# A two-layer graph network: the first expert layer scatters its rows by token, combining becomes plain, and work moves between stages

## The reference

```python
xn = LN(x)
# layer 0: attention over edges (8 heads) + linear attention, then 2 of 8 experts
g = leaky_relu(xr[dst] + xl[src], 0.2)          # xl, xr: projections of xn
alpha = einsum(g, att) + log(edge_weight)       # softmax over the edges of each dst
x = x + segment_sum(xl[src] * softmax(alpha), dst) + bias + linear_attention(xn)
t = LN(x)
mask = one_hot(top_k(t @ Wg + bg, 2)).sum()
x = x + sum_e mask[e] * (gelu(t @ W1[e] + b1[e]) @ W2[e] + b2[e])
# layer 1: two graph convolutions + linear attention with an MLP, then 1 of 8 experts
xn = LN(x)
x = x + relu(gcn(relu(gcn(xn, W1)), W2)) + mix(xn)
x = x + nan_to_num(capacity_expert(x))          # at most 977 rows per expert
```

## Time and profile before

| | |
|---|---|
| median of 3 runs | 5924.41 us (5920.71 to 5925.23) |
| profiled execution | 5924.94 us, its span 5923.2 us |
| TensorE busy | 4048.7 us, 68% of the span |
| GpSimd busy | 3097.9 us, 52% |
| VectorE busy | 2628.5 us, 44% |
| ScalarE busy | 1112.7 us, 19% |
| mean granted TensorE clock | 0.749 of full speed |
| moved by DMA | 602.72 MB, mean 102 GB/s |

### The profile page before, as it was taken

How to read it: one execution, slowest core, us unless ns; L and a number is a source line. 1 busy time by engine, 2 the same in 40 slices (tenths; PEclk the granted TensorE clock), 3 DMA queues, 4 the chain that set the end, 5 groups by cost and what they waited for, 6 DMA issues and landing times. The chain is left out here.

```text
span 5923.2 us, 82263 instructions
## 1 busy us (share of the span) xinstructions
PE 4048.7 (68%) x19460; PEld 3300.3 (56%) x19461; DVE 2628.5 (44%) x5923; ACT 1112.7 (19%) x2524; POOL 3097.9 (52%) x3161
## 2 busy tenths in 40 slices
PE   4788999999469965089934555555455555592998
PEld 3577888888447744067734444444444444461665
DVE  5333333333689975034444434444433334342443
ACT  0122222222159921022210000000000000021121
POOL 1166767676248831500066777777677777603111
PEclk9889888888679985599955556666555555555999
DMA  5365555565248843342242111111211111122220
GB/s 197 94 183 182 180 178 181 177 181 177 70 157 273 272 135 108 122 125 64 62 122 54 32 32 33 33 33 30 44 33 32 33 32 34 28 72 81 84 79 31
DMA packets 414884, 602.72 MB, mean 102 GB/s; under 512 B 97612, under 2 KB 305118, under 8 KB 413351
## 3 DMA queue, kind: packets, MB, share of 16 engines
q1 hardware_dynamic: 283019, 348.08, 17.8%
q0 software_dynamic: 107056, 200.91, 14.7%
q10 hardware_dynamic: 24732, 52.87, 2.6%
HBM read 392.17 MB, written 221.97 MB: 104 GB/s over the span
## 5 line engine op out<-in xcount | busy, mean ns | idle before, releaser
L1867 POOL DMA_INDIRECT big<-t_d,src_tiles x1564 | 1497.9, 958 | 552.2 <-issue 462.5
L2090 PE MATMUL v_bank<-big,v_oh 128*128 x3328 | 682.9, 391 | 926.4 <-POOLq L1863 861.6
L2090 PEld LDWEIGHTS v_bank<-big,v_oh 128*128 128x128 f32 x3328 | 649.6, 299 | 1004.0 <-issue 1004.0
L640 POOL DMA_INDIRECT se_xj<-xl_d,se_idx x832 | 833.8, 1002 | 371.9 <-issue 193.0
L1945 DVE TENSOR_TENSOR big<-big,v_bank 128x64 f32 x1664 | 367.8, 221 | 1158.0 <-PE v_bank L2090 922.8
L737 PE MATMUL se_z_ps<-big,se_oht 128*128 x1664 | 543.4, 455 | 73.1 <-issue 45.7
L683 DVE TENSOR_TENSOR se_z<-se_z_ps,se_xj 128x528 f32<-128x528 f32 x416 | 293.3, 705 | 584.8 <-DMA se_xj<-xl_d,se_idx 450.3
L976 POOL TENSOR_TENSOR ae_v<-ae_v,ex 128x1792 f32<-128x1792 f32 x104 | 334.2, 3217 | 243.0 <-DMA ae_v<-xj_d 242.8
L759 PEld LDWEIGHTS se_al_ps<-atta,se_zt 128*128 128x128 f32 x3328 | 459.3, 214 | 0.0
L759 PE MATMUL se_al_ps<-atta,se_zt 128*128 128x8 f32 x3328 | 444.5, 260 | 0.0
L1017 PE MATMUL ae_bank<-ae_v,ae_oh 128*128 128x266 f32 x1664 | 401.1, 396 | 51.4 <-DVE big L1001 37.4
(11 more groups left out here) (406 smaller groups left out, 5916.6 us busy)
## 6 DMA issues: line engine op xcount, KB each, us to landing
xj_d<-se_xj SPq DMA_DIRECT2D x208, 528.0 KB, 3.4
ae_v<-xj_d SPq DMA_DIRECT2D x208, 528.0 KB
big<-t_d,src_tiles POOLq DMA_INDIRECT x1564
buf_d<-e_blank ACTq DMA_DIRECT2D x4, 4112.0 KB, 35.7
e_xs<-buf_d SPq DMA_DIRECT2D x106, 128.0 KB
y_d<-e_y SPq DMA_DIRECT2D x106, 128.0 KB
se_xj<-xl_d,se_idx POOLq DMA_INDIRECT x832, 3.1
v_xt<-xnt_d SPq DMA_DIRECT2D x98, 128.0 KB
```

Of the source, the lines that this page charges most:

```text
L640: nc.gpsimd.indirect_dma_start(half_of(u)[:, k, :], None, table, bass.IndirectOffsetOnAxis(ap=idx[:, u, k:k + 1], axis=0)).then_inc(landed ...
L1867: nc.gpsimd.indirect_dma_start(rows[:, t % RING, :], None, table, bass.IndirectOffsetOnAxis(ap=m.srct[:, t:t + 1], axis=0)).then_inc(lande ...
L2090: last = nc.tensor.matmul(bank[u][:, k * MH:(k + 1) * MH], oh[:, u, k, :], of_block(rows, at[k]), start=True, stop=True)
```

## The change

- Start: the nine projection weights are loaded by `load_projections` on ScalarE's queue in `edge_steps`, behind x and ahead of the zeroing. The read-back of the tables moves to the start of `project_nodes` on SyncE. `buf0_d` has rows of TW = 258: the last two columns, 1e6 in the blank, are to hold a token and an expert.
- Score stage: TensorE reads four block numbers at every second `expand` instead of two at each.
- Normalise stage: GpSimd makes the blank tile and SyncE blanks `buf1_d` there (and the pad rows of `y0_d`).
- Route, layer 0: each scattered row carries its token and its first expert; `erow` keeps the expert of each tile as floats on all partitions; `m.back` is gone.
- First experts: VectorE's `index` computes, two tiles ahead of the bias, where each row of a tile goes: its token, plus NP = 6272 if the tile's expert isn't the row's first. GpSimd scatters each y tile to `y0_d` (2 x NP rows) with that index. SyncE only loads; a load waits for the index of the tile that held the buffer. Rows of a blank have an index out of bounds and aren't written. The blanking is gone.
- Combine: SyncE loads each group's rows of both halves of `y0_d` in two plain DMAs; GpSimd does nothing.

The diff, cut to its core (lines "..." stand for what is left out; left out are declarations, and the context):

```diff
@@ -177,13 +178,16 @@
-        rowsin, stored, floats = m.sem("es_rowsin"), m.sem("es_stored"), m.sem("es_floats")
+        rowsin, floats = m.sem("es_rowsin"), m.sem("es_floats")
...
+        m.weighted = nc.alloc_semaphore(name="weighted")
+        stored = m.stored
...
-        zeros = m.ex[:, 2 * NT:2 * NT + ZT * D]
+        zeros = m.ex[:, 2 * NT:2 * NT + ZT * TW]
...
@@ -213,17 +217,11 @@
-                sp.dma_start(m.key_d.rearrange("(j p) e -> p j e", p=P), fd[:, :, :]).then_inc(stored, 16)
+                sp.dma_start(m.key_d.rearrange("(j p) e -> p j e", p=P), fd[:, :, :]).then_inc(m.keyed, 16)
...
-                sp.wait_ge(stored, 64)
-                sp.dma_start(m.btab, m.btab_d[0:NS].rearrange("(a n) -> a n", a=1)).then_inc(stored, 16)
-                sp.dma_start(m.stab, m.stab_d[0:NS].rearrange("(a n) -> a n", a=1)).then_inc(stored, 16)
-                ends_of_groups = m.need_d[0:NS].rearrange("(g k) -> k g", k=GS)[GS - 1:GS, :]
-                sp.dma_start(m.need, ends_of_groups, allow_slow_non_contiguous=True).then_inc(stored, 16)
-                sp.wait_ge(stored, 112)
...
@@ -232,13 +230,14 @@
-                act.wait_ge(zeroset, 1)
+                load_projections(act, m, a)
+                act.wait_ge(zeroset, 2)
...
-                    act.dma_start(m.buf0_d[b0 * P:b1 * P, :].rearrange("(p b) d -> p (b d)", p=P), zeros[:, 0:(b1 - b0) * D]).then_inc(zeroed, 16)
+                    act.dma_start(m.buf0_d[b0 * P:b1 * P, :].rearrange("(p b) d -> p (b d)", p=P), zeros[:, 0:(b1 - b0) * TW]).then_inc(zeroed, 16)
...
@@ -267,7 +266,9 @@
-                nc.vector.memset(zeros, 0.0).then_inc(zeroset, 1)
+                blank = zeros.rearrange("p (b d) -> p b d", d=TW)
+                nc.vector.memset(blank[:, :, 0:D], 0.0).then_inc(zeroset, 1)
+                nc.vector.memset(blank[:, :, D:TW], 1.0e6).then_inc(zeroset, 1)
...
@@ -419,6 +420,27 @@
+def load_projections(act, m, a):
+    wl, wr, wlt, wrt, bl, br, bcol, attc = m.projections
+    for out, w in ((wl[:, :, 0:D], "L0_gnn_W_l"), (wr[:, :, 0:D], "L0_gnn_W_r"), (wlt[:, :, :], "W_lT"),
...
+        act.dma_start(out, a[w].rearrange("(c p) n -> p c n", p=P)).then_inc(m.weighted, 16)
+    for out, w in ((bl[:, 0:D], "L0_gnn_b_l"), (br[:, 0:D], "L0_gnn_b_r")):
+        act.dma_start(out, a[w].partition_broadcast(P)).then_inc(m.weighted, 16)
+    for out, w in ((bcol[:, 0, :], "L0_gnn_b_l"), (bcol[:, 1, :], "L0_gnn_b_r")):
+        act.dma_start(out, a[w].rearrange("(c p) -> p c", p=P), allow_slow_non_contiguous=True).then_inc(m.weighted, 16)
+    act.dma_start(attc[:, :], a["L0_gnn_att"].rearrange("h c -> (h c)").rearrange("(c p) -> p c", p=P), allow_slow_non_contiguous=True).then_inc(m.weighted, 16)
...
@@ -454,14 +473,11 @@
-                for out, w in ((wl[:, :, 0:D], "L0_gnn_W_l"), (wr[:, :, 0:D], "L0_gnn_W_r"), (wlt[:, :, :], "W_lT"),
...
-                    sp.dma_start(out, a[w].rearrange("(c p) n -> p c n", p=P)).then_inc(s["weights"], 16)
...
+                sp.wait_ge(m.stored, 48)
+                sp.dma_start(m.btab, m.btab_d[0:NS].rearrange("(a n) -> a n", a=1)).then_inc(m.stored, 16)
+                sp.dma_start(m.stab, m.stab_d[0:NS].rearrange("(a n) -> a n", a=1)).then_inc(m.stored, 16)
+                ends_of_groups = m.need_d[0:NS].rearrange("(g k) -> k g", k=GS)[GS - 1:GS, :]
+                sp.dma_start(m.need, ends_of_groups, allow_slow_non_contiguous=True).then_inc(m.stored, 16)
...
@@ -476,6 +492,7 @@
+                sp.wait_ge(m.stored, 96)
...
@@ -491,7 +508,8 @@
-                dve.wait_ge(s["weights"], 16 * 9)
+                dve.wait_ge(m.weighted, 16 * 9)
+                dve.wait_ge(m.keyed, 16)
...
@@ -732,9 +752,10 @@
-                    blocks = blocks_of(nc, m, mybir.EngineType.PE, q * 2, 2)
+                    if v % 2 == 0:
+                        blocks[:] = blocks_of(nc, m, mybir.EngineType.PE, q * 2, 4)
...
-                        last = nc.tensor.matmul(z_ps[v % 2][:, i, 0:LW], oht[:, u, k + i, :], of_block(m.xr, blocks[i]),
+                        last = nc.tensor.matmul(z_ps[v % 2][:, i, 0:LW], oht[:, u, k + i, :], of_block(m.xr, blocks[2 * (v % 2) + i]),
...
@@ -787,6 +809,21 @@
+            @block.gpsimd
+            def _(pool):
+                nc.gpsimd.memset(blank[:, :, 0:RW - 1], 0.0).then_inc(s["blank"], 1)
+                nc.gpsimd.memset(blank[:, :, RW - 1:RW], 1.0e6).then_inc(s["blank"], 1)
+            @block.sync
+            def _(sp):
+                sp.wait_ge(s["blank"], 2)
+                slots = m.buf1_d.rearrange("(q p b) d -> q p b d", p=P, b=16)
+                for q in range(NE * CT // 16):
+                    sp.dma_start(slots[q], blank[:, :, :].to_broadcast([P, 16, RW])).then_inc(s["blanked"], 16)
+                for e in range(2):
+                    sp.dma_start(m.y0_d[e * NP + N:(e + 1) * NP, :], blank[0:NP - N, 0, 0:D]).then_inc(s["blanked"], 16)
+                sp.wait_ge(s["blanked"], NE * CT + 32)
...
@@ -1331,8 +1368,8 @@
                     if layer == 1:
...
-                        pool.wait_ge(s["t_ready"], 2 * (g + 1))
-                        pool.sem_inc(s["issued"], 1)
+                    pool.wait_ge(s["t_ready"], 2 * (g + 1))
+                    pool.sem_inc(s["issued"], 1)
                     pool.wait_ge(s["indexed"], pairs * (g + 1))
...
@@ -1366,6 +1403,7 @@
+                    c.did(V.tensor_scalar(first[:, :], m.tmp1[:, :], float(NE), None, ALU.add))
...
@@ -1456,9 +1493,9 @@
-                    if v % 7 == 0 and layer == 1:
-                        V.tensor_copy(disp[:, v // 7, :, 2 * D], m.prob[:, bass.ds(g * 7, 7)]).then_inc(s["t_ready"], 1)
-                        V.tensor_copy(disp[:, v // 7, :, 2 * D + 1], token[:, bass.ds(g * 7, 7)]).then_inc(s["t_ready"], 1)
+                    if v % 7 == 0:
+                        for at, what in ((RW - 2, m.prob), (RW - 1, token)) if layer == 1 else ((TW - 2, token), (TW - 1, first)):
+                            V.tensor_copy(disp[:, v // 7, :, at], what[:, bass.ds(g * 7, 7)]).then_inc(s["t_ready"], 1)
...
@@ -1528,14 +1565,14 @@
-        xs, xt = sb("xs", [P, 2, D]), sb("xt", [P, 2, D])
+        xs, xt = sb("xs", [P, 2, TW]), sb("xt", [P, 2, D])
+        which, idx = sb("which", [P, T0]), sb("idx", [P, T0], U32)
...
-        blank = sb("blank", [P, 1, RW])
...
-                                           "y_made y_ready blank blanked").split()}
+                                           "y_made y_ready chosen indexed issued").split()}
...
@@ -1544,18 +1581,21 @@
                 def load(j, u, r):
...
+                        sp.wait_ge(s["indexed"], j - 1)
...
-                def store(j, u, r):
-                    sp.wait_ge(s["y_ready"], j + 1)
-                    sp.dma_start(m.y0_d[bass.ds(j * P, P), :], y[:, u, :]).then_inc(y_out[u], 16)
-                pipeline(sp, T0, 2, (0, load), (6, store))
-                for u in range(2):
-                    sp.wait_ge(y_out[u], 16 * T0 // 2)
+                pipeline(sp, T0, 2, (0, load))
...
+                def index(j, u, r):
+                    dve.wait_ge(x_in[u], 16 * (r + 1))
+                    V.tensor_scalar(which[:, bass.ds(j, 1)], xs[:, u, TW - 1:TW], m.erow[:, bass.ds(j, 1)], float(NP),
+                                    ALU.not_equal, ALU.mult).then_inc(s["chosen"], 1)
+                    dve.wait_ge(s["chosen"], j + 1)
+                    V.tensor_tensor(idx[:, bass.ds(j, 1)], which[:, bass.ds(j, 1)], xs[:, u, TW - 2:TW - 1], ALU.add).then_inc(s["indexed"], 1)
...
@@ -1584,20 +1624,21 @@
                         dve.wait_ge(y_out[u], 16 * r)
                     V.tensor_tensor(y[:, u, :], y_ps[u][:, 0:D], of_block(b2, e), ALU.add).then_inc(s["y_ready"], 1)
-                pipeline(dve, T0, 2, (0, bias1), (1, turned), (2, bias2))
+                pipeline(dve, T0, 2, (0, index), (2, bias1), (3, turned), (4, bias2))
...
-                nc.gpsimd.memset(blank[:, :, 0:RW - 1], 0.0).then_inc(s["blank"], 1)
-                nc.gpsimd.memset(blank[:, :, RW - 1:RW], 1.0e6).then_inc(s["blank"], 1)
+                for j in range(T0):
+                    pool.wait_ge(s["indexed"], j + 1)
+                    pool.sem_inc(s["issued"], 1)
+                    pool.wait_ge(s["y_ready"], j + 1)
+                    nc.gpsimd.indirect_dma_start(m.y0_d, bass.IndirectOffsetOnAxis(ap=idx[:, j:j + 1], axis=0), y[:, j % 2, :], None,
+                                                 bounds_check=2 * NP - 1, oob_is_err=False).then_inc(y_out[j % 2], 16)
+                for u in range(2):
+                    pool.wait_ge(y_out[u], 16 * T0 // 2)
...
-                act.wait_ge(s["blank"], 2)
-                slots = m.buf1_d.rearrange("(q p b) d -> q p b d", p=P, b=16)
-                for q in range(NE * CT // 16):
-                    act.dma_start(slots[q], blank[:, :, :].to_broadcast([P, 16, RW])).then_inc(s["blanked"], 16)
...
@@ -1610,7 +1651,6 @@
-                act.wait_ge(s["blanked"], NE * CT)
...
```

(26 more changed lines are left out.)

64 lines of the change are left out of this document (34 added, 30 removed).

## The result

| | before | changed |
|---|---|---|
| median, 18 runs each | 5922.23 us | 5857.18 us |
| ratio | | 0.9895, 95% interval 0.988 to 0.9911 |
| profiled execution | 5924.94 us, span 5923.2 | 5862.27 us, span 5860.6 |

The change takes 65.0 us (1.1%) off the median and 62.7 off the profiled executions. Since barriers cut the program, the difference can be read stage by stage: a stage ends with the last semaphore event of its block line. Lengths in us, one profile each; the third column is a second profile of the changed kernel, made later together with other runs (the median of the kernel before: 5911.68 us there). A lone profile of an untouched stage can be off by several us: the aggregate stage, which no edit touches, shows 465.5, 472.6 and 464.5.

The account below looks back on a forecast made before the run. Each barrier-separated stage has its own bound: TensorE in the first experts, GpSimd's gathers in scores, VectorE's chain in normalise. Stage terms sum to -60.8, so 5924.9 - 60.8 = 5864 us, range 5842 to 5892.

Parts of the forecast that it names:

- Projection: Projection stage: weights already loaded, so VectorE waits only for GpSimd's masks, 88.29 - 81.56, 6.7 us saved.
- First stage: Edge steps: the tables' wait no longer closes the stage, which ends at 75.5 instead of 79.9, 4.4 us earlier.
- the sum of 4.7 us on ScalarE's queue: First stage: weights ahead of the zeroing make ScalarE's wait end at 70.5 + 4.7 + 0.3 = 75.5.
- done by 75: First stage: VectorE finishes by 75, so ScalarE's wait at 75.5 ends the stage.
- Score stage: Block numbers read by four: quicker TensorE gives part of the 9.8 us that gathers wait for se_z; -4 us.
- The phase rival: Score stage: VectorE's one-hot meets gathers in another phase, 20 us less or 35 more; chance 0.12, half each way.
- Normalise and route: Normalise: 55 us of blanking hidden beside VectorE's chain, 0. Route, layer 0: small copies and GpSimd waits, +0.8 us.
- First expert stage, its start: Without ScalarE's 32.30 us of issuing blanks, first up matmul at 2500.2, -28.5 us; late loads, another -2.0.
- the bound of -32: First expert stage's start: the larger-gain limit for -28.5 and -2.0 together; the other limit was -25.
- full DMA cost 2.0 us: First expert stage's start: a few loads come late while DMA is full of blanks, estimated at half a tile of 4.10.
- Its middle and its end: First expert stage: index and scatters fit free room, 0; at the end GpSimd's drain +8.7 and last scatter +1.1.
- Combine: Combine stage: plain loads start the first chain 12.0 us earlier and remove 13.8 us of VectorE's later waits; -25.8 us.

Follow-up runs that it names:

- without pauses: Sets of runs in which GpSimd does not pause after every sixteenth gather; the kernel before takes 5911.68 and 5930.88 us.
- With pauses: Sets of runs in which GpSimd pauses 3 to 4 us after every sixteenth gather; the kernel before takes 6450.67 and 6489.03 us.

## Why the prediction was right, and where it was not

The forecast was 5864 us; the profiled execution took 5862.27, the median is 5857.18. That the first is so near is partly luck: in that profile two stages that nothing was forecast for moved by +7.1 (aggregate) and -4.4 us (attention's finish), the first stage fell 3.6 short, and the score stage and the expert stage's start each gave 3 more than their terms. The total itself repeats: 0.9896 in the other set without pauses. Part by part:

- **The start.** Projection: forecast -6.7, measured -6.5 and -6.3 (two more profiles without pauses have 157.5 and 159.4 us, which is -6.4 and -4.5). First stage: forecast -4.4, measured -0.8 and -1.6. The step that failed is the sum of 4.7 us on ScalarE's queue with VectorE "done by 75". ScalarE's wait ended at 79.1 and 78.2, not at 75.5. Nor was VectorE done by 75, for its edge rows come late: at 65.35 and 66.89 in two profiles without the move, at 67.8 to 69.1 with it, so that VectorE ended up to 3 us later. With the zeros gone and x held they came at 61.70 and the stage took 71.0; with the weights behind the zeroing they were hardly earlier. So the zeroing's writes hold them up. Why they come 1 to 4 us later than in the kernel before is open: the weights' place isn't it, and the wider rows of the zeroing were not tried alone.
- **Score stage.** Forecast -4. By two against by four in one set without pauses: 3.5 us, one profile each. The term fits that; the -7.2 of the first two profiles holds wander as well. The phase rival (up to +35 or -20) didn't come: the gathers' mean went from 1002 to 994 ns. With pauses the same part is worth 34 us, which the prediction had no row for.
- **Normalise and route.** 0 and +0.8 forecast, 0 to -1.0 and +0.4 to +0.6 measured. 29.7 MB of writes left the normalise stage at 117.3; 30.8 MB, of which 14.0 in rows of 1032 bytes, made it 120.5.
- **First expert stage, its start.** The tail's +9.2 taken from the total of -24.3 leaves -33.5, against -28.5 - 2.0, and outside the bound of -32. The first up matmul came 26.6 us earlier, not 28.5; the rest, 6.9, is what full DMA and the clock cost behind it, which was put at 2.0. So the number nearly held, and the mechanism did not. I wrote that issuing the blanking holds ScalarE, and let full DMA cost 2.0 us. The runs show the reverse: with ScalarE free and DMA full the last bias2 started 27.2 us later than in the changed kernel, and only 6.3 earlier than in the kernel before, where ScalarE was held as well. The hold hid behind late loads. Both went with the blanking, so the sum came out: luck, in this term. Had the change only moved the issue to another queue, the forecast would have been wrong by most of 28.5.
- **Its middle and its end.** 0 and +9.8 forecast. TensorE stayed at 380.00 of 380. Last bias2 to stage end was 482.8 - 479.7 = 3.1 us before and 458.5 - 446.2 = 12.3 after: +9.2. That this drain goes by the number of indirect DMAs is shown by halving them.
- **Combine.** Forecast -25.8, measured -26.5. First sum at 8.9 us where 8.6 was forecast.

## What to carry to other kernels

Cut a program with barriers at them and price each stage alone; then a wander of 7 us in an untouched stage isn't taken for an effect. When a bulk write shares a stage with small loads, ask first what full DMA does to the loads, not who issues it: move it to a stage whose DMA is idle, or spread it. Count the indirect DMAs of a stage, since GpSimd pays for them again at its end; whether that lengthens the stage depends on whether GpSimd is the last to finish.

## What the runs showed of the hardware that I had not expected

- Behind landed scatters GpSimd's DRAIN takes 82 to 83 ns per indirect DMA of the stage: 4383 ns for 53, 5286 for 64 in the second expert stage, 8712 for 106, beside 4061 and 8067 for 49 and 98. It doesn't go on like that: a convolution issues 782, and its drain is 9.0 us. A drain can also begin while gathers are still being issued and then holds their time too: 22.2 us in the old combine stage with 98 gathers, from 3107.1, of which 8.6 lie behind the last gather's end. From the source line of the convolution's block in the changed kernel:

```profile
L1887 POOLq DRAIN  x2: 9037/9037/9037, 4084.8 to 5110.4; - x2
```

- Full DMA is no shared resource on equal terms: 60 us of it left TensorE 128 matmuls instead of 223, while some 63 GB/s of the same writes cost nothing. The Trainium skill (DMA: Bandwidth & Descriptors, "Queues, rings and completion order") says that each DMA engine takes turns between queues in whole packets. By that a load on one queue should advance beside blanks on another; the trace shows that it does, but with waits of up to 9.53 us for one load of 129 KB.
- Rows of 1032 bytes were written at 226 to 234 GB/s, the same buffer in rows of 2064 bytes at 352. It isn't that rows of 1 KB are too short: zeros for `y0_d`, in rows of 1024 bytes, went at 340 to 343 (the normalise stage of the run with plain stores and GpSimd's blanking):

```profile
1540.00:1550.00 10.00, 0.00 (x0) 0.00 (x0) 9.93 (x4) 0.00 (x0) 0.00 (x0) 0.50 1.04 342
```

  The Trainium skill (DMA: Bandwidth & Descriptors, "How a descriptor splits into AXI transactions") says that a descriptor that begins at a multiple of 256 bytes is cut into transactions of 256 and one for what is left over, and that the first transaction of any other begins at the boundary below it. The measurements agree in sign: 1024 bytes leave nothing over and 1032 leave 8. Whether the eight bytes left over or the rows' shifted beginnings cost more, no run tells.
- The kernel before takes 5911 to 5931 us in some sets of runs and 6450 to 6489 in others, one chip having shown both; GpSimd's pauses go with the long ones. With them the change is worth more (0.9808 against 0.9895), as the reads of block numbers count there, and as the old combine stage took 202.1 us (the kernel before with block numbers by four) instead of 169.8. Where the pauses come from no run here shows.
